# A routed feed-forward block counted in half tiles: 20 tiles for 23, a tile table by small products, FP32 first layer in the early tiles

## The reference, cut to what matters

```python
x = x + tanh(g_xattn) * xattn(ctx, ctx, layernorm(x))      # 16 sequences of 64 tokens, D = 128
z = layernorm(x)                                           # 1024 tokens
probs = softmax(z @ gate_w.T)                              # 8 experts
topk_probs, topk_idx = top_k(probs, 2)                     # 2048 (token, expert) slots
h = gelu(w1[expert] @ z + b1[expert])                      # 128 -> 512
y = w2[expert] @ h + b2[expert]                            # 512 -> 128
x = x + tanh(g_ffn) * sum over the 2 choices of y * prob
```

## Time and profile before

| | |
|---|---|
| median of 3 runs | 92.72 us (92.6 to 92.79) |
| profiled execution, its own time | 92.59 us |
| its span, first to last instruction | 90.8 us |
| busy: PE, PEld | 77.7, 64.4 us |
| busy: DVE, ACT, POOL | 65.4, 57.0, 51.2 us |
| granted TensorE clock | 1.0 over the whole span |

### The profile page before, as it was taken

How to read it: one execution, slowest core, us unless ns; L and a number is a source line. 1 busy time by engine, 2 the same in 40 slices (tenths; PEclk the granted TensorE clock), 3 DMA queues, 4 the chain that set the end, 5 groups by cost and what they waited for, 6 DMA issues and landing times.

```text
span 90.8 us, 2765 instructions
## 1 busy us (share of the span) xinstructions
PE 77.7 (86%) x841; PEld 64.4 (71%) x841; DVE 65.4 (72%) x307; ACT 57.0 (63%) x173; POOL 51.2 (56%) x82
## 2 busy tenths in 40 slices
PE   4997898887898966999849999999999999999800
PEld 1375466574363443899739999999999999999700
DVE  2079737999999899999987767569787467436760
ACT  4166689984949598799537887577567657732000
POOL 6975499006787778772000189777877784400650
PEclk9999999999999999999999999999999999999999
DMA  1999999690212103551362345521210120138443
GB/s 23 297 369 414 426 447 433 218 332 2 66 59 66 59 29 115 150 146 40 85 148 66 84 126 144 139 69 34 66 34 20 38 65 13 46 90 221 158 129 102
DMA packets 11662, 12.65 MB, mean 139 GB/s; under 512 B 1379, under 2 KB 10615, under 8 KB 11392
## 3 DMA queue, kind: packets, MB, share of 16 engines
q1 hardware_dynamic: 9840, 9.74, 33.1%
q0 software_dynamic: 1120, 2.12, 7.2%
q10 hardware_dynamic: 688, 0.61, 2.5%
HBM read 8.18 MB, written 4.48 MB: 139 GB/s over the span
## 4 chain that ended last, share of the span: by engine, by line
DVE 38%; PE 35%; DMA 11%; issue 4%; POOL 4%; SPq 2%; POOLq 1%; ACT 1%; DVEq 0%
PE bank L834 17%; DVE hot L951 6%; DMA res<-results 5%; PE bank L816 4%; PE bank L818 4%; PE bank L817 4%; DMA x_sb<-in_x 4%; DVE x L975 3%; DVE w_lo L1077 2%; DMA results<-y_sb,in_rows 2%; PE bank L800 2%; SPq L365 2%; POOL rstd L413 2%; DVE stats L982 2%; DVE xn L911 2%
## 5 line engine op out<-in xcount | busy, mean ns | idle before, releaser
L614 ACT ACTIVATE hid<-bank,wp 128x128 f32<-128x128 f32 x92 | 26.2, 368 | 14.4 <-PE bank L818 14.4
L460 POOL DMA_INDIRECT results<-y_sb,in_rows x19 | 19.3, 1016 | 16.7 <-ACT y_sb L570 10.4
L834 PE MATMUL bank<-w_sb,hid 128*128 (+1 forms) x184 | 25.6, 282 | 0.0
L834 PEld LDWEIGHTS bank<-w_sb,hid 128*128 128x128 f32 x184 | 22.4, 192 | 0.0
L376 POOL DMA_INDIRECT dispatched<-rows,slot x16 | 16.0, 998 | 9.4 <-DVE slot L1044 5.2
L816 PE MATMUL bank<-xs_t,w_hi 128*128 128x128 f16 x76 | 13.8, 219 | 0.0
L817 PE MATMUL bank<-xs_t,w_hi 128*128 128x128 f16 x76 | 13.8, 219 | 0.0
L818 PE MATMUL bank<-xs_t,w_lo 128*128 128x128 f16 x76 | 13.8, 219 | 0.0
L636 PE MATMUL bank<-ones 128*128 128x512 bf16 x38 | 12.1, 438 | 1.3 <-DVE ones L898 1.3
L1151 DVE COPY xs_t<-bank 128x256 f16<-128x256 f16 x19 | 5.5, 292 | 8.9 <-PE bank L800 8.6
L816 PEld LDWEIGHTS bank<-xs_t,w_hi 128*128 (+1 forms) x76 | 7.4, 98 | 0.1
(11 more groups left out here) (174 smaller groups left out, 164.6 us busy)
## 6 DMA issues: line engine op xcount, KB each, us to landing
w_sb<-in_w SPq DMA_DIRECT2D x2, 2048.0 KB, 11.1
in_rows<-dispatched SPq DMA_DIRECT2D x23, 65.0 KB, 1.9
results<-zeros SPq DMA_DIRECT2D x1, 1024.0 KB, 5.0
res<-results SPq DMA_DIRECT2D x4, 256.0 KB, 3.9
dispatched<-pad_rows SPq DMA_DIRECT2D x9, 65.0 KB
ctx_sb<-in_ctx_t SPq DMA_DIRECT2D x1, 512.0 KB, 5.3
wp<-in_wpack ACTq DMA_DIRECT2D x1, 342.0 KB, 3.5
results<-y_sb,in_rows POOLq DMA_INDIRECT x19
```

The source lines that it names most:

```text
L460: pool.indirect_dma_start(results_dram, bass.IndirectOffsetOnAxis(ap=in_rows[:].bitcast(U32)[:, t, TARGET:TARGET + 1], axis=0), y_sb[:, t, ...
L614: mm = act.activation(hid[:, t % HIDS, b, :], hid_ps[h % len(hid_ps)][:, (b % HALVES) * P:(b % HALVES + 1) * P], ACT.Gelu_apprx_tanh, bias ...
L834: mm = pe.matmul(to, hid[:, t % HIDS, b, :], w2_sb[:, e, b * P:(b + 1) * P], start=False, stop=b == BLOCKS - 1)
```

## The change: what it does

Slots are counted in parts of 64. The first half tile of every expert is in the early tiles: tile t below 4 holds the first 64 slots of expert 2t and of expert 2t+1, side by side. Tiles 4 to 7 ("mixed") hold two further half tiles, of any two experts, taken from registers; their second w2 comes by a DMA of its own into `w2_second`. Tiles 8 to 19 are whole tiles of one expert. In tiles 0 to 7 each product of `hidden` becomes two with 64 moving columns, each product of `output` two whose stationary operand has 64 columns and whose results go to partitions 0 to 63 and 64 to 127, and each gelu two with 64 columns.

The table is made with small products on PE (`segments`, `find_tiles`) and short DVE work on 8 or 16 partitions between them, all of it ahead of the slots of the last group; before, DVE made it behind the one-hots. The one-hots are made by 3 instructions a tile (`HOT_CHUNKS`), not 8, and compare in FP32. Tiles 0 to 3 run their first layer in FP32 from `w1_sb`; so the low parts of w1 are wanted from tile 4 on, and all eight pieces are made behind the one-hots (one of them stood at 27.3 in `TIMES`). The rows of tiles 0 to 7 are loaded by two DMAs of 64 rows each.

```diff
-N_TILES = (SLOTS - EXPERTS) // SLOT_TILE + EXPERTS
-FURTHER = N_TILES - EXPERTS
-EARLY = 4
+N_TILES = -(-((SLOTS - EXPERTS) // PART + EXPERTS) // 2)
+EARLY = MIXED = EXPERTS // 2
+SHARED = EARLY + MIXED
+WHOLE = N_TILES - SHARED
+FURTHER = 2 * MIXED + WHOLE
+IN_FP32 = 4
+HOT_CHUNKS = [(0, 4), (4, 6), (6, 8)]
...
-    W1_LOW: [27.3],
+    W1_LOW: [],
...
+            sp.wait_ge(table_ok, 3)
+            for u in range(0, 2 * MIXED, LOADS):
+                of = table_values(sp, tile_experts, EXPERTS - 1, u)
+                for i in range(1, LOADS, 2):
+                    k = (u + i) // 2
+                    sp.dma_start(w2_second[:, k, :], w2[:, bass.ds(of[i], 1), :]).then_inc(ld_second[k], 16)
+            first = []
+            for u in range(0, FURTHER, LOADS):
+                first += table_values(sp, tile_rows, PAD_ROW, u)
             sp.wait_ge(sent, 16 * (SLOTS // P))
...
+            for t in range(EARLY, SHARED):
+                load_shared(t)
+                load_shared(t - EARLY)
+            for t in range(SHARED, N_TILES):
+                sp.dma_start(in_rows[:, t, :], rows_dram[bass.ds(first[2 * MIXED + t - SHARED], SLOT_TILE), :]).then_inc(loaded[t], 16)
...
+                    for part, i in entries(t):
+                        to = hid_ps[h % len(hid_ps)][:, at + part.start:at + part.stop]
+                        e = experts[i]
+                        if t < IN_FP32:
+                            mm = pe.matmul(to, w1_sb[:, e, f], xs_f[:, t, part], start=True, stop=True)
+                        else:
+                            hi, lo = xs_t[:, t % XS, 0, part], xs_t[:, t % XS, 1, part]
+                            pe.matmul(to, w1_hi[:, e, f], hi, start=True, stop=False)
+                            pe.matmul(to, w1_hi[:, e, f], lo, start=False, stop=False)
+                            mm = pe.matmul(to, w1_lo[:, e, f], hi, start=False, stop=True)
...
+                    for part, i in entries(t):
+                        if EARLY <= t < SHARED and part.start:
+                            weights = w2_second[:, t - EARLY, f]
+                        else:
+                            weights = w2_sb[:, experts[i], f]
+                        mm = pe.matmul(to[part, :], hid[:, t % HIDS, b, part], weights, start=False, stop=b == BLOCKS - 1)
...
                 if g == GROUPS - 1:
                     places(g)
-                    counted()
-                    one_hots(0, 0, STARTS[2])
-                    pads()
+                    pads(g)
+                    count_tiles()
+                    lane_made = lanes()
+                    one_hots(0, 0)
+                    locate()
                     rows_low(2)
-                    one_hots(0, STARTS[2], STARTS[3])
+                    one_hots(0, 1)
                     rows_low(3)
-                    one_hots(0, STARTS[3])
+                    one_hots(0, 2)
+                    table(lane_made)
                     gates(g)
                     slots(g)
...
-            for t in range(EARLY, EARLY + LAG):
-                split_rows(t)
+            for t in range(EARLY, EARLY + LAG + 1):
+                if t >= IN_FP32:
+                    split_rows(t)
             for t in range(EARLY, EARLY + LAG):
                 copy_rows(t)
-            split_rows(EARLY + LAG)
-            low_weights(5)
```

More of the change, by code:

```diff
@@ L316, in tokens, with loads_of, entries @@
             return slice(STARTS[g] * P, STARTS[g + 1] * P)
+        def loads_of(t):
+            return 32 if t < SHARED else 16
+        def entries(t):
+            return [(slice(i * PART, (i + 1) * PART), 2 * t + i) for i in range(2)] if t < SHARED else [(slice(0, SLOT_TILE), EXPERTS + t)]
         def table_values(engine, table, largest, t):
@@ L731, in ranks, with into @@
                 n = SIZES[g]
[L733 to L734 removed]
+                columns = n + (g == GROUPS - 1)
+                def into(j, to=columns):
+                    return turn[g % 2][:, RANK + j * EXPERTS:RANK + to * EXPERTS]
                 def counted(u, j):
[L737 to L739 removed]
@@ L740, in ranks @@
-                mm = pe.matmul(into(0), ones[:], region_row[:, 0:n, :], start=False, stop=n == 1 and g == 0)
+                    return chosen[:, u, None, :].to_broadcast((P, columns - j, EXPERTS))
+                pe.matmul(into(0), ones[:], region_row[:, 0:columns, :], start=True, stop=False)
+                mm = pe.matmul(into(0, n), before[:], chosen[:, group(g), :], start=False, stop=columns == 1 and g == 0)
                 for u in range(STARTS[g]):
-                    mm = pe.matmul(into(0), ones[:], counted(u, 0), start=False, stop=n == 1 and u == STARTS[g] - 1)
@@ L743, in ranks, with count @@
-                for j in range(1, n):
-                    mm = pe.matmul(into(j), ones[:], counted(STARTS[g] + j - 1, j), start=False, stop=j == n - 1)
+                    mm = pe.matmul(into(0), ones[:], counted(u, 0), start=False, stop=columns == 1 and u == STARTS[g] - 1)
+                for j in range(1, columns):
+                    mm = pe.matmul(into(j), ones[:], counted(STARTS[g] + j - 1, j), start=False, stop=j == columns - 1)
                 mm.then_inc(rank_ps, 1)
-            def gather(e):
-                if e == 0:
+            def count():
+                for t in range(TILES):
+                    mm = pe.matmul(table_bank[0:EXPERTS, COUNT:COUNT + 3 * EDGES], chosen[:, t, :], ones[:, 0:3 * EDGES],
+                                   start=t == 0, stop=t == TILES - 1)
+                mm.then_inc(count_ps, 1)
@@ L763, in count @@
-            def count():
-                for t in range(TILES):
-                    mm = pe.matmul(count_bank[:, COUNT:COUNT + EXPERTS], ones[:], chosen[:, t, :],
-                                   start=t == 0, stop=t == TILES - 1)
-                mm.then_inc(count_ps, 1)
+                if i >= 2:
+                    pe.wait_ge(first_ok, i - 1)
+                for k, (a, b) in enumerate(HOT_CHUNKS):
+                    pe.wait_ge(hot_ok, i * len(HOT_CHUNKS) + k + 1)
+                    for t in range(a, b):
+                        if i == 0 and t in STARTS:
+                            pe.wait_ge(low_ok, STARTS.index(t) + 1)
+                        for c in range(2):
+                            mm = pe.matmul(gather_ps[i % 2][:, 0:P], rows_16[:, t, c, :], hot[:, i, t, :, :],
+                                           start=t == 0 and c == 0, stop=t == TILES - 1 and c == 1)
```

355 lines of the change are left out of this document (198 added, 157 removed).

## The result

The changed kernel takes 104.72 us in the median of four runs (103.78 to 105.41), the kernel before 92.75 in the same comparison. The ratio is 1.126, 95% interval 1.116 to 1.137. 98.5 had been forecast, 100.5 at most: the sign was right, the time is outside the range.

A forecast was written before the change was run, and what follows sets the result against it. PE was taken as bound by row loads until tile 4 starts, then by its sequencer's register work in the mixed tiles: 5.9 + 5.3 - 5.35 = +5.9 on 92.59 gives 98.5 us, range 94.0 to 100.5.

The forecast's parts named there:

- Three tiles fewer, -5.35: Whole tiles: 20 instead of 23 at 1.784 us each saves 5.35 us.
- The early tiles: 16 passes of 0.112, outputs of 1.2: Tiles 0 to 3 on PE: FP32 first layer 1.79 us, bound by weight columns; second layer with bias and drain 1.2.
- Halves side by side: Second layer on PE: two 64-column halves run at once, 8 pairs at about 0.112 us each, 0.90; otherwise 1.8.
- rule on the tiling mode: Changing tiling mode drains PE: 0.25 us a tile with lost prefetch, in all 8 shared tiles; without it, forecast 0.25 lower.
- X = 53.05: Start of tile 4's first layer, set by tile 6's tenth row load landing at 52.1; 5.9 us later than 47.14.
- PE is through with hidden(3) at 51.4: PE's early tiles: done at 51.4; turn and copy add 0.7, so tile 4 could start at 52.1, under the loads' date.
- POOL's extra setup lies ahead of its first send, where it waits for DVE: GpSimd's added setup operations: covered by its wait for VectorE.
- POOL is idle by then: GpSimd at the last slots (38.6): idle, so the last four sends go from 38.9, the last at 42.7 instead of 40.51.
- The mixed tiles, +5.3, a block 0.235: Tiles 4 to 7: sequencer's register work bounds PE, eight blocks of 0.235 us, 3.2 a tile (first 2.8); +5.3 us.
- The rival in which the register work hides: Mixed tiles run at PE's own 2.05 us each, total 94.3 us; chance 0.16.
- the faster one: Half tile costs no more than a whole, mixed tiles 1.784 us, no drain or register wait; 93.1 us; chance 0.08.
- Tail unchanged: From the last scattered tile to the end, scatter, reload and sums stay as they were: change 0.

The follow-up runs named there:

- version 7: version 6 with each early tile's FP32 first layer in four products of 128 columns with one expert; 98.12 us, ratio 1.052.
- version 4: The changed kernel with the first-layer weights of tiles 4 to 7 at fixed addresses, so their results are of other experts; 99.58 us, ratio 1.060.
- version 1: The changed kernel with products nobody reads put where TensorE waits; 102.97 us, ratio 1.106.
- version 6: version 3 with tiles 4 to 7 each in one load of 128 rows and no fills behind the turning; 99.41 us, ratio 1.072.
- version 8: The kernel before the change, with twelve small GpSimd operations added behind its last constant; 95.29 us, ratio 1.010.
- version 12: version 3 with two fills behind the turning and VectorE's gates and slots of the last group ahead of the tile table; 99.55 us, ratio 1.075.
- version 3: The changed kernel with fills where TensorE waits (four behind the turning) and the loads of tiles 4 to 7 ahead of tiles 0 to 3; 99.31 us, ratio 1.070.
- version 5: version 3 with the first-layer weights of tiles 4 to 7 at fixed addresses (results of other experts); 96.33 us, ratio 1.040.
- versions 9: version 3 with SyncE's 1 MB clearing issued when the second group's slots are there instead of at 15.5; 99.91 us, ratio 1.077.
- 13 (none): version 12 with the clearing moved as well, GpSimd's constants partly ahead of its wait, and no fills behind the turning; 101.10 us, ratio 1.091.

## Why the prediction was right in sign and wrong in size

Point by point, in its own terms:

- *Three tiles fewer, -5.35*: right.
- *The early tiles: 16 passes of 0.112, outputs of 1.2*: right at the full clock (3.87 a tile for 3.89), and version 7 shows the ground given for it, the weight load. *Halves side by side*: right; two halves start 0.01 apart (62.49 and 62.50 in the changed kernel), and an output with its bias takes 1.05, from 48.22 to 49.27, for the 1.2 taken. The Trainium skill's rule on the tiling mode (TensorEngine Tiling (Array Packing), Key Properties) that the prediction weighed agrees with the trace: in version 4 the transpose behind an output comes 0.2 behind its last pair (62.37 behind 62.16), while the pairs follow each other in 0.11.
- *X = 53.05*: this step failed; it measured 56.64. What it had as the mechanism (tile 6's tenth DMA) is what the trace shows, but four of its sizes were off, by 3.6 together: the last send at 43.71 for 42.7 (+1.0), held by slots that came 0.8 late, of which 0.55 was the clock (next point; they start at 38.87 in version 1); the first load 2.88 behind it for 2.5 (+0.4); 7.2 us from the first to the tenth issue for 4.5 (+2.7, of which some 1.6 is the price of a load, taken from loads of 128 rows, where one of 64 costs the queue more (version 6), 0.7 a slow one of 1.31, which the prediction had set aside ("most of that mean is a few slow ones"), and 0.4 a gap on the queue); and 1.95 from there to the landing, for the 2.4 taken (-0.5).
- *PE is through with hidden(3) at 51.4*: this failed too, and silently. TensorE's clock was taken as granted at 1.0, as the profile of before had it. The change puts six tiny products and a wait of 0.81 behind the last fills, where the first gather had followed at once (at 33.81), and the early tiles then ran at 1.2 GHz up to 45.1: through with hidden(3) at 55.0. With the clock kept (version 1) it is 51.8, so the rest of this path was right within 0.4. The error stayed under the loads' 56.5, as version 1 shows (X moved by 0.18), and still cost 1.6 us: 0.6 of it between X and the last y_sb, where the second stretch at 1.2 GHz lies. In the Trainium skill (TensorE: Matmul & The Clock Gate, HAM oscillation — how this bites in real kernels) stands that waits between stretches of products bring the clock down in the middle of a kernel. The trace agrees, with 0.50 granted behind both waits and a mean of 0.99 once they are filled; the waits of the page's example are longer than the 0.81 and 1.27 here.
- *POOL's extra setup lies ahead of its first send, where it waits for DVE*: wrong. Twelve operations that look covered moved the first send by 1.9 us (version 8), so GpSimd waits there for something that is not VectorE's slots; no row names it. *POOL is idle by then*: true, but with only 0.65 us to spare at the last slots; from a first send at 20.93, as before, it would have been 2 or more. It cost X nothing here, and took away what earlier slots could have given (version 12).
- *The mixed tiles, +5.3, a block 0.235*: right in the sum. X to the last y_sb is 0.4 longer with three tiles fewer, so this part costs +5.75, the second stretch at 1.2 GHz included; with the clock kept it is 5.1 (version 1) and 4.95 (version 3). Versions 4 and 5 show that it is the addresses: 3.0 to 3.3 us go with the first layer's alone. The parts were wrong, and that they cancel is luck. With the clock kept (version 3) the four tiles take 12.3 for 12.4, but only tile 4 has all its blocks at 0.235; in tiles 5 to 7 four or five blocks go at 0.09 first, and the eighth starts 0.9 to 1.1 us behind the first, not 1.65. From there to the next tile it takes 1.75 to 1.99, where the forecast left 1.15 in tile 4 and 1.55 in the others. Together the first part is 1.9 us less than forecast and the second 1.8 more. The forecast spread the sequencer's work over the first layer; TensorE meets it partly there and partly at the second layer, since with fixed addresses (version 5) that second part falls to 1.36 (tiles 4, 5 and 7). The rival in which the register work hides is out, and so is the faster one, in which a half tile costs no more than a whole.
- *Tail unchanged*: off by 1.3, 0.6 of it GpSimd's backlog of scatters by the rows. Sixteen of them at 1.3 us start 13 us later than before (64.93 for 51.90), because ScalarE's gating of tiles 0 to 3 stands behind the activations of tiles 5 to 8, which come later with X (9.5) and with the mixed tiles, and never quite catch up. It was not thought of since GpSimd was not near the end's chain before.

The net: with the clock kept and the loads in the old order (version 3) the same change takes 99.3, inside the forecast's own range of 96.8 to 100.2. The sums for TensorE's work held, the mixed tiles' in part by luck; what the forecast lacked is what waiting does to the clock, and what a DMA's issue costs. None of the versions of the changed kernel reaches the 92.7 of the kernel before: removing the first layer's register work as well leaves 96.3.

## What to carry to other kernels

A tile that is cut in halves saves rows, but doubles whatever is paid per instruction: register addresses at 0.235 us a block, DMA issues at 0.6 to 0.7 us each (more than the 0.52 of a whole tile's load), FP32 passes at the price of their weights. Count those first, not the rows. Where a change puts tiny products or a wait into TensorE's stream, look whether the granted clock survives it, and put products that nobody reads there; the time lost at 1.2 GHz may be hidden under another wait, as here, and a later wait can bring a second fall that is not. And where two bounds lie within 1 us of each other (here loads at 56.5, TensorE at 55.5), test them together: one alone gave a third of what both gave.

## What the runs showed of the hardware that I had not expected

- The clock fell behind 1.5 us with 0.67 busy, and stayed low through 10.3 us with 9.80 busy (34.8 to 45.1); the second time it was back after 3.4 us with 3.18 busy. The fills did not always keep it: in versions 9 (four behind the turning), 12 (two) and 13 (none) TensorE ran at 1.2 GHz for 3.4 us from 55.9, 55.9 and 54.6 on.
- The sequencer's address work bounds TensorE only once it has been caught up: behind a second layer the first four or five blocks of a first layer follow in 0.09 us each and the rest in 0.235. In the second stretch at 1.2 GHz (tile 5), behind a second layer that took 1.95, no block took more than 0.18.
- A load of 64 rows holds SyncE's queue longer than one of 128: 0.47 to 0.57 us for 0.33 with an address from a register, 0.60 for 0.43 with a fixed one. In nearly every profiled execution one or two loads of such a series take 0.8 to 1.6.
- In the changed kernel GpSimd's first indirect send waits 3.6 to 4.3 us behind its last setup operation with nothing recorded, 2.8 if the 1 MB clearing is not in flight. What it waits for is open.
